# A perceiver layer on one core: GpSimd instead of VectorE makes the low halves of the self attention's projection weights

## The reference, cut to what matters

```python
x = x + xattn(layernorm(x), ctx, ctx, Wq, Wk, Wv, Wo)   # cross attention, 32 heads, 8 key/value heads
x = x + attn(layernorm(x), Wq, Wk, Wv, Wo)              # causal self attention with rope over 32 rows
x = x + layernorm(x) @ dequantised_3bit(weight).T + bias
```

## Time and profile before

| what | value |
|---|---|
| median of 3 runs | 364.55 us (363.93 to 364.71) |
| the profiled execution's own time | 363.73 us |
| its span, first to last instruction | 361.9 us |
| PE busy | 339.8 us, 94% |
| DVE busy | 232.2 us, 64% |
| ACT busy | 203.2 us, 56% |
| POOL busy | 104.4 us, 29% |
| mean granted TensorE clock | 0.986 |

### The profile page before, as it was taken

How to read it: one execution, slowest core, us unless ns; L and a number is a source line. 1 busy time by engine, 2 the same in 40 slices (tenths; PEclk the granted TensorE clock), 3 DMA queues, 4 the chain that set the end, 5 groups by cost and what they waited for, 6 DMA issues and landing times.

```text
span 361.9 us, 8398 instructions
## 1 busy us (share of the span) xinstructions
PE 339.8 (94%) x2962; PEld 246.0 (68%) x2962; DVE 232.2 (64%) x420; ACT 203.2 (56%) x371; POOL 104.4 (29%) x195
## 2 busy tenths in 40 slices
PE   8999778999999999999999999998788989999996
PEld 4855546777777777777777777765366748875664
DVE  2977655766766766766757667657845237886652
ACT  4543226667757766676776677567656622275310
POOL 1432813133133133132241331330103141551410
PEclk9999898999999999999999999999998999999999
DMA  7970597575776486785876886979200000000002
GB/s 280 395 94 4 98 216 179 141 110 176 166 109 177 125 147 168 126 154 156 130 150 148 119 217 153 157 183 128 26 2 0 2 2 0 1 2 0 2 29 87
DMA packets 35820, 41.25 MB, mean 114 GB/s; under 512 B 15136, under 2 KB 30496, under 8 KB 33696
## 3 DMA queue, kind: packets, MB, share of 16 engines
q1 hardware_dynamic: 35360, 40.74, 52.5%
q10 hardware_dynamic: 432, 0.13, 0.1%
HBM read 24.07 MB, written 1.05 MB: 69 GB/s over the span
## 4 chain that ended last, share of the span: by engine, by line
PE 80%; DVE 7%; ACT 3%; DMA 2%; SPq 2%; issue 2%; POOL 2%; ACTq 0%; DVEq 0%; POOLq 0%
PE b_c L1089 8%; PE b_d L1030 8%; PE b_s L1051 7%; PE b_v L1005 4%; PE b_c L1234 4%; PE b_v L1007 4%; PE b_v L1006 4%; PE b_k L1007 4%; PE b_k L1005 4%; PE b_k L1006 4%; PE b_x L977 3%; PE b_t L977 3%; DMA kstack<-kparts 2%; PE b_c L1115 2%; PE b_c L1219 2%
## 5 line engine op out<-in xcount | busy, mean ns | idle before, releaser
L763 DVE TENSOR_REDUCE negmax<-b_s 128x1 f32<-128x512 f32 x128 | 87.9, 687 | 70.4 <-PE b_s L1051 63.2
L572 ACT ACTIVATE region<-b_c 128x512 f32<-128x512 f32 x128 | 74.6, 597 | 56.3 <-PE b_c L1089 33.5
L1051 PE MATMUL b_s<-kstack,qstack 96*128 96x512 bf16 x128 | 50.0, 390 | 9.0 <-DVE negmax L763 4.7
L1089 PE MATMUL b_c<-qstack,kstack 108*128 108x128 bf16 x512 | 51.3, 224 | 2.0 <-ACT region L572 1.5
L1089 PEld LDWEIGHTS b_c<-qstack,kstack 108*128 108x128 bf16 x512 | 33.1, 99 | 28.3 <-issue 21.4
L469 POOL TENSOR_TENSOR mwide<-negmax,zeros 128x4 bf16<-128x4 f32 x32 | 6.4, 200 | 122.4 <-DVE negmax L763 122.4
L1005 PE MATMUL b_v<-cT_h,wkv_h 128*128 128x512 f32 x64 | 31.7, 495 | 0.0
L1030 PE MATMUL b_d<-region,vaug 128*17 128x128 f32 x1024 | 31.4, 275 | 0.0
L1005 PE MATMUL b_k<-cT_h,wkv_h 128*128 128x512 f32 x64 | 30.8, 481 | 0.0
L460 POOL TENSOR_TENSOR kparts<-kres,zeros 128x512 bf16<-128x512 f32 x16 | 18.9, 1182 | 38.5 <-DVE kres L748 38.5
L1030 PEld LDWEIGHTS b_d<-region,vaug 128*17 128x17 f32 x1024 | 26.8, 98 | 2.0 <-issue 0.2
(11 more groups left out here) (397 smaller groups left out, 682.7 us busy)
## 6 DMA issues: line engine op xcount, KB each, us to landing
cx<-in_ctx_dram SPq DMA_DIRECT2D x16, 1024.0 KB, 5.1
kstack<-kparts SPq DMA_DIRECT2D x96, 128.0 KB, 4.3
qstack<-region SPq DMA_DIRECT2D x76, 32.0 KB, 2.9
xs<-in_x_dram SPq DMA_DIRECT2D x1, 1024.0 KB, 7.9
region<-in_L_xattn_Wq_dram SPq DMA_DIRECT2D x1, 1024.0 KB, 10.1
cx<-in_L_xattn_Wo_dram SPq DMA_DIRECT2D x8, 128.0 KB, 5.2
cx<-in_L_attn_Wq_dram SPq DMA_DIRECT2D x1, 1024.0 KB, 5.9
region<-in_L_attn_Wo_dram SPq DMA_DIRECT2D x8, 128.0 KB, 7.2
```

The lines of the kernel that those rows point to most:

```text
L572: nc.scalar.activation(pT[:, g], b_c[g % 2][:].rearrange("p (a n) -> p a n", a=KT), ACT.Exp, scale=SCALE).then_inc(exp_ready, 1)
L763: nc.vector.tensor_reduce(negmax[:, n % 2, g:g + 1], b_s[:], AX, ALU.max, negate=True).then_inc(max_ready, 1)
L1051: nc.tensor.matmul(b_s[:], qstack[0:STACK, g, n % 4], kstack[0:STACK, n % 4, g], start=True, stop=True).then_inc(s_ready, 1)
L1089: last = nc.tensor.matmul(b_c[g % 2][:, P * a:P * a + P], kstack[0:ROWS, m % 4, g, P * a:P * a + P], qstack[0:ROWS, g, m % 4], start=True, ...
```

## The change

Six subtractions of 128x512, which VectorE made one at a time in six steps, are made by GpSimd in two blocks: the four query chunks behind `max_parts` of batch 14's first half in slot 14, the keys and values behind `max_parts` of batch 14's second half in slot 15. ScalarE's part, TensorE's part and all DMAs stand as before.

```diff
             def slot(n, trip):
                 if live(n - 1, trip):
                     max_parts(n - 1, 1, trip)
                 if splits_keys(n, 1, trip):
                     key_parts(n + 1, trip)
+                if n == B - 1:
+                    low_keys_values()
                 if live(n, trip):
                     max_parts(n, 0, trip)
+                if n == B - 2:
+                    low_queries()
                 for g in range(G):
                     early(n, g, steps)
+            def low_queries():
+                for c in range(C):
+                    pool.wait_ge(swq_high, c + 1)
+                    nc.gpsimd.tensor_tensor(swq_l[:, c], swq[:, c], swq_h[:, c].bitcast(F32), ALU.subtract).then_inc(swq_ready, 1)
+            def low_keys_values():
+                for i in range(2):
+                    pool.wait_ge(swkv_high, i + 1)
+                    nc.gpsimd.tensor_tensor(wkv_l[:, i], swkv[:, i], wkv_h[:, i].bitcast(F32), ALU.subtract).then_inc(swkv_ready, 1)
...
                         nc.vector.tensor_tensor(wT_l[:, c], b_tx[c % 2][:], wT_h[:, c].bitcast(F32), ALU.subtract).then_inc(wT_ready, 1)
-                    if (n, g) in SPLIT_AT:
-                        split_weights(SPLIT_AT[n, g])
                     early(n, g, steps)
```

More of the change, by code:

```diff
@@ L894, in transposed @@
                                         ALU.subtract).then_inc((xnT_ready, xnT2_ready)[norm], 1)
[L896 to L904, removed]
             def turn(src, a, b, shape, cs, sn, done):
```

## The result

Four runs of the changed kernel took 360.87 us in the median (359.9 to 361.66), four of the kernel before 364.63. The ratio is 0.9898, with an interval of 0.9866 to 0.9931: faster by 3.8 us. The profiled execution took 361.66 us, with a span of 359.9.

What follows compares the result with a forecast made beforehand. The prediction took VectorE's order to bound the stretch from 246.8 to 260.1 us. Its terms, 0.58 + 0.60 + 0.01 + 0.72 + 0.60 = 2.51 us, gave 364.55 - 2.5 = 362.05 us, range 361.1 to 363.8.

Steps and rivals of the forecast that it cites:

- Links 1 to 5: Chain of waits from step 4 of slot 14 to the residual: earlier by 0.58 us, growing to 2.51.
- the sum: Gain at the normalised tile: 2.51 us, less 0 to 1.3 where VectorE and GpSimd meet.
- links 1 to 3: Steps 4 to 6 of slot 14: maxima earlier by 0.58, then 1.18 us; scores and last query high half follow.
- links 4 and 5: From step 7 to the residual: `wT_l` earlier by 1.91 us, the residual by 2.51 without the last low half.
- Link 6: Statistics, square root and normalisation: ScalarE's table load loses nothing, so the tile starts at 257.00 instead of 259.51.
- What hides GpSimd: Six added subtractions, 7.6 us, fit GpSimd's 8.25 us idle time; it can be some 1.3 us late without harm.
- the slack at `max_rows`: On TensorE: `max_parts` on GpSimd ends at 254.2 and TensorE arrives at about 254.5, leaving 0.25 us.
- rival (b): At the tile: the normalisation meets GpSimd's last subtraction, costing up to 0.98 us; gain 1.5, time 363.0, chance 0.15.
- (a): At the residual: TensorE and ScalarE keep their old times, so only 1.19 us come back; 363.4, chance 0.14.
- (c): Behind 260 us: a wait of its own lets nothing reach the end; 364.2 to 364.9, chance 0.08.
- Rival (d): TensorE's low clock at 276 to 280 us moves or lasts longer: 365.3, chance 0.08; without the fall 360.8.
- a run's scatter of 0.4: Allowance of 0.4 us for run differences, put on top of the half-gain rivals' 363.4, giving the upper end 363.8.

Runs made afterwards that it cites:

- e3: The changed kernel plus six unread VectorE maxima over one 128x512 SBUF operand at the six old places: 363.34 us, ratio 0.9987 to the kernel before.
- e4: The changed kernel plus six unread VectorE subtractions of two 128x512 SBUF operands at the old places: 366.49 us, ratio 1.0091 to the kernel before.
- e1: Against the kernel before, GpSimd makes only the four query chunks, VectorE keeps the keys' and values' low halves: median 362.24 us, ratio 0.9951.
- e2: Against the kernel before, GpSimd makes only the keys' and values' low halves, VectorE keeps the four query chunks: median 362.22 us, ratio 0.9949.

## Why the prediction was right or wrong

**Links 1 to 5: right.** Each came out within 0.03 us: 0.61 at step 4 for 0.58 (the maximum started 0.42 after its scores, where 0.46 had been estimated), 1.20 at step 5 for 1.18, 1.92 at `wT_l` for 1.91, 2.52 at the residual for 2.51, 2.51 at the tile. One reading ahead of the links is short: the chain names four of the removed instructions and not two (246.87, 249.79, 254.82 and 256.63), of which those of 249.79 and 256.63 hold 0.6 us or more. The links count them all, so the sum isn't touched. The queries alone give what links 1 to 3 say, the keys and values alone what VectorE's order in links 4 and 5 says, and e3 takes the whole back by filling VectorE alone.

**Link 6: right.** The table load ended at 257.68 and the row that it serves came at 258.17 + 0.15; it was late by nothing.

**What hides GpSimd: right.** A subtraction took 1.27 us. `max_parts` was held up behind the fourth (254.93, with the last maximum's start at 253.27), the slack at `max_rows` was 0.23 us for 0.25 forecast, and the idle time behind it 1.10.

**The port, rival (b): didn't happen, and is real.** The margin was 0.33 us for 0.3. The one-column operation took 0.15 within GpSimd's subtraction (258.17, beside 255.91 to 258.46), so the 0.3 that was kept for it is nothing. The remark that all but one of VectorE's long instructions read PSUM overlooks the row statistics, which read the SBUF tile `xs` alone (257.22 here, within GpSimd's last subtraction); they took 0.70 us, as without it (0.69 before), so that one SBUF operand cost nothing. e4 shows the price where VectorE has two SBUF operands.

**Rivals (a) and (c): excluded** by the tile and by e1 and e2, which give what the feedback through TensorE and ScalarE demands. **Rival (d), the clock,** went the other way in this pair of profiles, by 1.36 us, as its last sentence allowed at 360.8. Its price of 1.3 came from the stretch of 276 to 280 us alone and left out that from 272, where the clock was 0.89; the pairs of profiles gave 1.4 to 1.6. That the clock is different in the next execution of the same kernel was not weighed into the range.

**The step that failed is the last one, from the sum to the median and its range.** The working took the three runs shown (363.93 to 364.71) for the scatter and put "a run's scatter of 0.4" on top. The scatter of one kernel is over 5 us from end to end. So the base of 364.55 was 1.1 us over the kernel's own median of 363.48, and a median of four runs on the other side could lie 1.5 us to either side of its own. 363.48 - 2.51 is 360.97, and the 31 runs gave 361.26 in the median. The lower end of 361.1 was too high, since it let in only a part of the clock's return, which the prediction itself had priced at 1.3. Three nearly equal runs were no evidence for a small scatter. What the runs showed in its place is a standard deviation of 1.5 us, with the wait for the keys' DMA in the opening (1.9 us) and the two places of low clock (0.6 to 1.7 and 1.4 to 1.6 us) behind it. The 1.3 us by which the four runs on each side showed more than the links hold are the draw of those runs and not the change, by the table above.

## What to carry to other kernels

Read the stretch and not the share: VectorE was 64% busy and 7% of the chain, and relief was still worth 2.5 us, since in 14 us of mixed work its order set TensorE's. An instruction moved to an idle engine brings what it held back, followed link by link with what was already late beside it; here the two halves of the change added up to less than the whole. And compare places in two traces from a mark ahead of the change, for a difference of 1.8 us from the opening or 1.4 from the clock can be as large as the effect. A range for a median of few runs has to hold that scatter.

## What the runs showed of the hardware

- GpSimd's subtraction of two float32 operands of 128x512 took 1.27 us beside a VectorE that reads PSUM or one SBUF operand, and VectorE's own stayed at 0.68. With two SBUF operands on both engines, 1.77 and 1.74 were the worst (e4). GpSimd's own small operations feel it too: 0.57 instead of 0.20 us beside a two-operand subtraction on VectorE.
- The granted clock falls to 1.2 GHz behind the same two idle times of TensorE in some executions and not in others (six of twelve profiles, none of six with the idle times filled), for some 3 us each time, at 1.4 to 1.6 us of the whole.
- The first scores of slot 1, which wait for a DMA, differ by 1.9 us in their start between executions of the same code.
